# Top 32 of the FiLM block: four heads and sixteen batches packed into tiles of 128 rows, and the mean over heads taken by fp32 products with token matrices

## What is computed

```python
B, T, H, DH, K_TOP = 16, 100, 4, 32, 32              # 1444 keys
scores = einsum('bthd,bghd->bhtg', Q, K) / sqrt(DH)   # Q = x Wq, K = ctx Wk
scores = where(vision_mask, scores, -inf)
topv, topi = top_k(scores, K_TOP)                     # the 32 largest of 1444
probs = softmax(topv)
attn = zeros.at[topi].set(probs)                      # 32 weights of 1444
attn_mean = attn.mean(over the 4 heads)
c_t = attn_mean @ (ctx Wv) * text_mask
# c_t then scales and shifts a layer norm of x, a convolution over tokens and a feed forward
```

## Time and profile before

| | |
|---|---|
| median of 3 runs | 5123.84 us |
| lowest and highest run | 5123.05 and 5160.94 us |
| span of the profiled execution | 5139.5 us |
| busy in that span: PE, DVE, ACT, POOL | 80%, 58%, 41%, 34% |
| DVE busy from 3804.7 to 4625.6 us | 820.07 of 820.90 us |
| MAX8 and MATCH_REPLACE8 of 100x1444 | 256 and 256 |

### The profile page before, as it was taken

One profiled execution on the slowest core, in us unless ns is written; L12 is line 12 of the kernel. 1 busy time (PEld: TensorE's weight loads), 2 busy tenths in 40 slices (PEclk: granted clock), 3 DMA queues, 4 the chain that ended last, 5 costly groups with the idle time before them and its releaser, 6 DMA issues. The chain is left out here.

```text
span 5139.5 us, 86857 instructions
## 1 busy us (share of the span) xinstructions
PE 4115.3 (80%) x26550; PEld 2846.4 (55%) x26550; DVE 2994.6 (58%) x4577; ACT 2115.7 (41%) x3227; POOL 1733.6 (34%) x1171
## 2 busy tenths in 40 slices
PE   8899999999979988778789999994763434336699
PEld 4588888888867746534445555552432222223377
DVE  4344445444523444446545676656459999996433
ACT  3255555555522232124324555542235555551122
POOL 2266666666524232004310000000225555541033
PEclk8799999999969988799867999996876666667699
DMA  2000000000002203220022222210010101000011
GB/s 85 1 10 19 10 19 19 19 10 19 10 1 62 59 1 91 48 61 2 1 56 47 65 62 62 62 33 1 1 24 18 26 17 26 17 19 1 0 61 48
DMA packets 124607, 152.80 MB, mean 30 GB/s; under 512 B 86912, under 2 KB 110224, under 8 KB 124080
## 3 DMA queue, kind: packets, MB, share of 16 engines
q1 hardware_dynamic: 124208, 147.72, 11.5%
HBM read 109.43 MB, written 2.66 MB: 22 GB/s over the span
## 5 line engine op out<-in xcount | busy, mean ns | idle before, releaser
L989 POOL TENSOR_TENSOR pexp_lo<-arena,pexp_hi 128x800 fp32r<-128x800 f32 x384 | 635.7, 1655 | 443.2 <-POOLq L988 442.5
L2173 DVE TENSOR_REDUCE arena<-ps 100x1 f32<-100x482 f32 (+1 forms) x768 | 489.9, 657 | 266.8 <-DVEq L2160 256.5
L2053 DVE TENSOR_REDUCE arena<-ps 128x1 f32<-128x482 f32 (+3 forms) x624 | 392.9, 656 | 365.6 <-DVEq L2031 354.8
L1330 ACT ACTIVATE arena<-ps 128x800 f32<-128x800 f32 x384 | 322.3, 839 | 500.3 <-ACTq L1328 497.8
L2471 DVE MATCH_REPLACE8 arena<-arena 100x1444 f32<-100x1444 f32 x256 | 420.8, 1656 | 0.0
L1420 ACT ACTIVATE arena<-ps 128x800 f32<-128x800 f32 x384 | 315.5, 837 | 249.8 <-ACTq L1419 243.6
L3202 PE MATMUL ps<-kst,qs 96*100 96x482 f32 (+1 forms) x768 | 376.2, 492 | 43.0 <-PEq L3156 39.4
L935 POOL TENSOR_TENSOR max_diag<-w_const,arena 100x800 fp32r<-100x800 f32 x160 | 246.8, 1543 | 436.5 <-POOLq L933 436.5
L3331 PE MATMUL ps<-w_const,w_cross 100*128 100x100 f32 x192 | 43.2, 380 | 374.1 <-PEq L3328 374.1
L1331 ACT ACTIVATE pexp_hi<-ps 128x800 fp32r<-128x800 f32 x384 | 319.5, 832 | 0.0
L2573 DVE TENSOR_TENSOR arena<-ps,arena 128x400 f32<-128x400 f32 x256 | 147.1, 575 | 280.2 <-DVEq L2572 280.2
(11 more groups left out here) (393 smaller groups left out, 9621.0 us busy)
## 6 DMA issues: line engine op xcount, KB each, us to landing
ctxT<-in_ctxT SPq DMA_DIRECT2D x56, 541.5 KB
kst<-mid SPq DMA_DIRECT2D x128, 180.5 KB, 3.1
ctxk<-in_ctx SPq DMA_DIRECT2D x40, 528.0 KB
chunk<-in_ff_chunks SPq DMA_DIRECT2D x77, 193.0 KB, 2.4
arena<-gate_dram SPq DMA_DIRECT2D x64, 200.0 KB, 3.8
kst<-xn SPq DMA_DIRECT2D x64, 180.5 KB, 2.9
arena<-gate_dram SPq DMA_DIRECT2D x64, 100.0 KB, 2.6
arena<-in_ctxT SPq DMA_DIRECT2D x8, 541.5 KB
```

What stands on the lines that cost most here:

```text
L989: own(nc.gpsimd.tensor_tensor(pexp_lo[p % 3][:, :, :], pexp[p % 3], pexp_hi[p % 3][:, :, :], ALU.subtract))
L1330: nc.scalar.activation(pexp[p % 3], of, ACT.Exp, scale=scale).then_inc(s.pexp_ready, 1)
L2053: peak = nc.vector.tensor_reduce(mparts[0:at.stop - at.start, m, c:c + 1], bank(k, z - a, at.stop - at.start), AX.X, ALU.max)
L2173: peak = nc.vector.tensor_reduce(mparts2[:, h, c:c + 1], bank(k, z - a, S), AX.X, ALU.max)
```

## The change

The 400 rows of a batch (4 heads x 100 tokens) are filled up to 13 groups of 32 rows (`QUADS`), and four groups of any batch make a tile of 128 rows: `TILES` = 16 x 13 / 4 = 52. Thirteen tiles hold four batches; a batch touches four tiles, and three of thirteen tiles hold rows of two batches. The scores of such a tile are made in two or three pieces (`pieces_of`: output at row 0, 32, 64 or 96). The four heads are no longer scaled and added up one by one. For each tile ACT scales a 0/1 matrix `picks` (128 rows x 100 tokens per batch) by 1/`den` to `by_den`, and PE multiplies the kept exponentials of the tile (128 rows x 128 keys as weights) with `by_den`, over the four tiles of the batch into one PSUM area: this sums heads, divides and turns in one. The transposes, the adds on POOL and the scaling of 1444 columns on ACT are gone. `picks` is a new input of 1600 columns, loaded once. The small products alternate between banks 6 and 7. PE, ACT, POOL and SP are written out without loops; DVE loops 12 times over two pairs.

```diff
+QUADS = -(-TH * S // 32)
+TILES = B * QUADS // 4
+RING = 7
+def first_tile(b):
+    return QUADS * b // 4
+def last_tile(b):
+    return (QUADS * b + QUADS - 1) // 4
# buffers
-    scores_sb = [shared([S, K]) for i in range(2)]
-    left = [shared([S, K]) for i in range(4)]
-    expd = [shared([S, K]) for i in range(4)]
-    attn = [w_cross[0:S, K * i:K * i + K] for i in range(2)]
+    scores_sb = [shared([128, K]) for i in range(2)]
+    left = [shared([128, K]) for i in range(4)]
+    by_den = [w_cross[:, ring_at + 2 * S * i:ring_at + 2 * S * i + 2 * S] for i in range(RING)]
+    expd = [shared([128, K]) for i in range(RING - 3)] + [w_cross[:, expd_at + K * i:expd_at + K * i + K] for i in range(3)]
# POOL
-            def pair(half, par):
...
-                    own(nc.gpsimd.tensor_tensor(expd[k], expd[k], left[k], ALU.subtract))
...
-                        own(nc.gpsimd.tensor_tensor(attn[par], attn[par], expd[k], ALU.add))
+            def kept(k):
...
+                own(nc.gpsimd.tensor_tensor(expd[k % RING], expd[k % RING], left[k % 4], ALU.subtract))
+                pool.sem_inc(s.kept_ready, 1)
# ACT, scale
-                    nc.scalar.activation(to, expd[k], ACT.Copy, scale=den[:, k:k + 1]).then_inc(s.scaled_ready, 1)
+                    nc.scalar.activation(by_den[k % RING][:, 0:cols], picks[:, pick_at(k):pick_at(k) + cols], ACT.Copy,
+                                         scale=den[:, k % 4:k % 4 + 1]).then_inc(s.scaled_ready, 1)
# ACT, order of the work
+            for n in range(TILES // 2):
+                exponents(n)
+                if n > 0:
+                    scale(n - 1)
+                if n + 1 < TILES // 2:
+                    scores(n + 1)
+                for b in range(B):
+                    if last_tile(b) // 2 == n - 1:
+                        mean(b)
+                for b in range(2, B):
+                    if first_tile(b) // 2 == n + 2:
+                        queries(b)
+                sums(n)
# DVE
-            with dve.Fori(0, B - 1) as i:
+            with dve.Fori(0, TILES // 4 - 1) as i:
                 pair(0)
                 pair(1)
# PE, scores
-                    ins = mm(bank(3 * (h % 2) + c, z - a, S), qv[:, h, :], ctxT[par][0:C + 1, a:z], start=True, stop=True)
+                    for b, j, q, n in pieces_of(k):
+                        ins = mm(ps[32 * j:32 * j + 32 * n, 3 * (k % 2) + c, 0:z - a], qv[b % 2][:, 32 * q:32 * q + 32 * n],
+                                 ctxT[b % 2][0:C + 1, a:z], start=True, stop=True)
# PE, mean
+                tiles = range(first_tile(b), last_tile(b) + 1)
...
-                        ins = nc.tensor.transpose(bank(6, S, r, t % 4 * S), attn[par][:, 128 * t:128 * t + r], ident[0:S, 0:S])
+                        for k in tiles:
+                            at = S * batches_of(k).index(b)
+                            ins = mm(bank(n, S, r, t % 4 * S), expd[k % RING][:, 128 * t:128 * t + r], by_den[k % RING][:, at:at + S],
+                                     start=k == tiles[0], stop=k == tiles[-1])
# PE, order: mean(b) with last_tile(b) // 2 == n - 1, queries, then
+                if n + 2 < TILES // 2:
+                    scores(2 * n + 4)
+                    scores(2 * n + 5)
```

More of the change, by code:

```diff
@@ L311, in film_parts, with batches_of, pieces_of, pick_at @@
                 skip=column(q["D_skip"]), mod=np.tile(q["mod_gate"].reshape(1, 1), (128, 1)))
+def first_tile(b):
+    return QUADS * b // 4
+def last_tile(b):
+    return (QUADS * b + QUADS - 1) // 4
+def batches_of(k):
+    return [b for b in range(B) if first_tile(b) <= k <= last_tile(b)]
+def pieces_of(k):
+    cuts = []
+    for j in range(4):
+        b, q = divmod(4 * k + j, QUADS)
+        if cuts and cuts[-1][0] == b and cuts[-1][1] != 1:
+            cuts[-1][3] += 1
+        else:
+            cuts.append([b, j, q, 1])
+    return cuts
+def pick_at(k):
+    return 100 * sum(len(batches_of(c)) for c in range(k % QUADS))
+def token_picks():
+    out = np.zeros((128, pick_at(QUADS - 1) + S * len(batches_of(QUADS - 1))), np.float32)
+    for k in range(QUADS):
+        for r in range(128):
+            b, q = divmod(4 * k + r // 32, QUADS)
+            at = 32 * q + r % 32
+            if at < TH * S:
+                out[r, pick_at(k) + S * batches_of(k).index(b) + at % S] = 1
+    return out
 def pack(parts):
@@ L1449, in own, with queries, side_bank, scores @@
                 act.sem_inc(s.act_done, -1)
-            def queries():
+            def queries(b):
                 act.wait_ge(s.proj_full, 1)
                 act.sem_inc(s.proj_full, -1)
-                own(nc.scalar.activation(qv[0:C, :, :], bank(6, TH * S, C).rearrange("p (h t) -> p h t", t=S), ACT.Copy))
+                own(nc.scalar.activation(qv[b % 2][0:C, 0:TH * S], bank(side_bank(), TH * S, C), ACT.Copy))
                 act.sem_inc(s.proj_free, 1)
                 act.sem_inc(s.qv_ready, 1)
-            def scores(half):
+            count = [0]
+            def side_bank():
+                count[0] += 1
+                return 6 + (count[0] - 1) % 2
+            def scores(n):
                 for i in range(2):
@@ L3344, in mean @@
                 pe.sem_inc(s.uv_ready, -1)
-                pe.wait_ge(s.proj_free, 1)
-                pe.sem_inc(s.proj_free, -1)
-                mm(bank(6, S), W("tk", "wv"), uv, start=True, stop=True).then_inc(s.proj_full, 1)
-            def batch(b, par, first=False):
-                if not first:
-                    mean(1 - par)
-                queries(b + 1)
-                for h in range(TH):
-                    scores(h, 1 - par)
-            queries(0)
-            for h in range(TH):
-                scores(h, 0)
-            batch(0, 0, first=True)
-            with pe.Fori(0, B // 2 - 1) as i:
-                batch(2 * i + 1, 1)
-                batch(2 * i + 2, 0)
-            mean(0)
-            mean(1)
+                mm(bank(side_bank(), S), W("tk", "wv"), uv, start=True, stop=True).then_inc(s.proj_full, 1)
+            queries(0)
+            scores(0)
+            scores(1)
+            queries(1)
+            scores(2)
+            scores(3)
+            for n in range(TILES // 2):
+                for b in range(B):
+                    if last_tile(b) // 2 == n - 1:
+                        mean(b)
+                for b in range(2, B):
+                    if first_tile(b) // 2 == n + 2:
+                        queries(b)
+                if n + 2 < TILES // 2:
+                    scores(2 * n + 4)
+                    scores(2 * n + 5)
+            mean(B - 1)
             layernorm(mid)
```

195 lines of the change are left out of this document (98 added, 97 removed).

## The result

The changed kernel takes 4998.05 us in the median of 4 runs (4964.83 to 5032.57), the kernel before 5142.39 us in 4 runs: ratio 0.9722, 95% interval 0.9669 to 0.9776. It is faster, and inside the range. The point, 4976 us, was worked out from a median of before of 5123.84 in three runs; a fourth run of before raised that median by 18.6 us. The forecast as a ratio, 0.9711, lies in the interval.

A forecast was written before the change was run, and what follows sets the result against it. VectorE, busy without a gap in the search for the 32 largest, was taken to bound the kernel. -153.7 us for fewer tiles, +5.7 at the end and 0 elsewhere gave -148.0: 5123.84 to 4976 us, range 4955 to 5030.

The forecast's parts named there:

- What bounds it: In the search for the 32 largest, VectorE is busy 820.07 of 820.90 us and sets the length.
- part 1: VectorE's passes: 64 tiles become 52, with rows free, saving 12 x 12.81 = 153.7 us.
- Part 3, the deadline: From a pair's start t, the sums behind the mean come at t + 31.7, wanted at t + 35.15: 3.4 us to spare.
- an inversion behind an idle time of over 1 us: Sign of being wrong: VectorE's inversion was never to stand behind idle time of over 1 us.
- the step for two means in a row: In five cases two means follow each other: 0 to 2 us for all five together, taken as 0.
- Part 4: Start 0 us; end, from the last pair's start F to the last copy, 60.5 us for 54.7, net +5.7.
- the forecast's case: Whole kernel at 4976 us, covering 4962 to 4990 us; chance 0.77.
- the late clock: Clock rises late or second of two means is late: 1 to 4 us wait per mean, 4991 to 5036; chance 0.11.
- By rows: VectorE's passes cost by rows: +32.8 us, +5.7 at the end, 5162 us; chance 0.03.
- Accumulated products that wait for each other: The mean's products into the same PSUM columns wait: up to 36 us per mean, about 5290 us; chance 0.03.
- It does not do what it says: VectorE already waits for another engine, so fewer passes would not shorten the stretch; no chance of its own stated.
- The clock at half: TensorE stays at 1.2 GHz through the mean's products: VectorE waits 6.3 us in 15 pairs, 5089 us; chance 0.05.

The follow-up runs named there:

- Experiment 1: Changed kernel with 16 instead of 13 groups of 32 rows per batch, so again 64 tiles of 128 rows: 5146.97 us, ratio 1.0021 to the kernel before.
- experiment 2: Changed kernel with VectorE's passes and the exponential of what is left on rows 0 to 99 of each tile only: 5009.27 us in one run.
- Experiment 3: Changed kernel with every product of the mean made twice, result unchanged: 5154.33 us, ratio 1.0019 to the kernel before.
- Experiment 4: Changed kernel with only the first of each batch's four tiles multiplied in the mean: 4961.8 us in one run.
- experiment 5: Changed kernel with the mean's products taking only rows 0 to 63 of each tile: 5135.47 us; only rows 0 to 79: 5140.6 us.
- experiment 7: Changed kernel with seven VectorE passes a tile for eight: 5073.92 us; with the sums moved earlier 5012.95; with single compare, sums earlier still, 4938.67 us.

## Why the prediction was right

**What bounds it, and part 1.** Right. VectorE has next to no gap, a pair is 25.61 us at 128 rows as at 100, and 12 tiles of 12.81 us went. Experiment 1 shows that nothing else in the change gains more than 1.4 us, experiment 2 that rows are free. The stretch is 151.1 us shorter and not 153.7, since two pairs are 1.5 and 1.7 us long.

**Part 3, the deadline.** Right in kind, and near in size: start of the products t + 10.6 (10.8 forecast), their length to the end of the last record 14.0 us (13.4), sums out at t + 32.3 (31.7), inversion at t + 35.1 (35.15). The clock came up after 6.3 us and not 4.7; the context products took 2.44 us (2.55). The slack is 2.8 us, not 3.4. Of the five places where two means follow each other two waited, 3.2 us together, where I had taken 0 and allowed 2. By one of my own signs of being wrong, an inversion behind an idle time of over 1 us, this shows: 1.2 and 1.3 us in the pairs, and 4.8 at the end. It cost little, but the step for two means in a row was too hopeful. Experiment 3 put 9 us on the chain and got pairs 6.6 to 7.6 us longer, about what the slack of 2.8 leaves. Experiment 4 took 8 us off and got 2.8 us in all the pairs together.

**Part 4.** The start cost nothing: from the first mask's start to the first MAX8 it is 12.4 us (3820.50 to 3832.91), for 12.25 before. The end was forecast at 60.5 us and took 60.0: TensorE began at F + 40.9 (41.3) and the burst took 13.4 us, as forecast. It was the mean of batch 14 in the last pair that set this start; experiment 1, without it, began at F + 34.9.

**The sum.** -148.0 forecast, -145.6 measured in the block; of the 2.4 us that are missing about 3 are the two waits, and half a microsecond comes back at the end. That the ratio came out within 0.0011 is luck, since its interval reaches 0.005 to either side. The median itself, 4998.05, lies outside the 4962 to 4990 that I gave to the forecast's case, and inside the 4991 to 5036 of the late clock. Only the block, and the median of before that rose by 18.6 us, say that it was the forecast's case.

**The rivals.** By rows: refuted by experiment 2. Accumulated products that wait for each other: refuted by 0.11 us a record at full clock in the burst of the profile. *It does not do what it says*: refuted by the pace of the pairs, with 12 tiles less. The clock at half: it did not happen, but experiment 5 shows that it was the rival to fear. It was priced at 95 us of waits and 18 more at the end; with the clock really held down, it is 127.8 in the stretch and 18.2 at the end, 146 us, as much as the whole gain. The pairs with two means cost up to 18.8 us each, and I had priced all fifteen alike. My reason against it, the 64 rows of the burst at 212.9 us, held for 64 and for 80 rows against 128. Whether tiles of 100 rows would have kept the clock down is not shown: no run has such products. The forecast rested on a choice between two rows, and the wrong one would have cost all of the gain.

## What to carry to other kernels

Where one engine is busy without a gap, count its passes: packing partial tiles pays by the tiles saved, and what leaves the other engines pays nothing as long as they keep their deadlines. For whatever is put on those others, trace the chain to the next place where the full engine waits for it and compute the slack, once for the usual round and once for two in a row; up to the slack it is free, and what goes beyond it is paid in each round. When the full engine gets faster, all these deadlines move up with it: recompute them and the pace of the next engine. In experiment 7 the block grew by 79 us with one pass less; moving the sums gave 74 of them back, and only with the cheaper compare, and the sums one copy earlier still, did the pass that was saved show. And fewer rows in a product are no saving if the clock stays down with them.

## What the runs showed of the hardware

- Back-to-back fp32 products with 128 columns of weights and 100 moving, 96 records: with 128 rows the clock rose within the burst (0.50 for 6.3 us, then 0.98; 13.8 us from first to last start); with 64 and with 80 rows it stayed at 0.50 through most bursts, 19.9 to 20.2 us each. Three bursts of 64 rows that began at 1.00 ran so for 4.2, 6.1 and 7.3 us and then fell to 0.50; two bursts of 80 rows kept it for their 10.7 us.
- The recorded length of one and the same MAX8 or MATCH_REPLACE8 drifted between 1.65 and 1.85 us along one execution (mean 1.72; 1.65 in most others), while their starts stayed 25.61 us a pair apart. Take a pace from starts.
- GpSimd on 128 x 1444 fp32: two-input subtract or multiply 3.25 us, a compare with a scalar per row 3.93, compare and multiply in one 5.15. A row of 1 x 1444 (from 8-bit numbers) with two operations takes 5.08, nearly as long as 128 rows.
- Two executions of one kernel differed by 60 us ahead of the block, with a clock of 0.87 and 0.95 over 870 us of it.
